# Summing the 16 states of a Mamba scan by accumulating DMAs issued from GpSimd (and the edges, the top two and the clamps by other instructions)

## Chip, cores and metric

One core of a Trainium2 chip, float32 data throughout. The metric is device microseconds of one launch. Three runs of the kernel before gave 5624.48, 5624.8 and 5625.91 us.

## What is computed

Input x is 4 sequences of 2048 tokens of 512 channels. One layer, with six modulation rows made from a small condition vector:

```python
h = layernorm(x) * (1 + ca) + sa
x = x + ga * mamba(h)
h = layernorm(x) * (1 + cb) + sb
x = x + gb * moe(h)          # 8 experts, the top two of 8 sigmoid scores, and one shared expert

# mamba: z = h @ W_in; val, gate = split(z); val = silu(conv3(val)); B, C, Delta from val
def step(h, inp):
    a_t, b_t, c_t, u_t = inp
    h = a_t * h + b_t * u_t[..., None]
    y_t = jnp.sum(h * c_t[:, None, :], axis=-1)     # the sum over 16 states
    return (h, y_t)
# out = y * silu(gate) @ W_out + residual
```

The recurrence runs over 2048 tokens for 512 channels with 16 states each. The change touches the sum over states, the gate times y, the 3-tap convolution's edges, the clamps on Delta, and the choice of the top two experts.

## The kernel before

**Tiling.** Tokens go in 16 blocks of 512 (`NQ`). The recurrence goes in 32 units (`NU`) of 128 channels by 1024 tokens. Each unit has 16 states (`N`), so there are 512 states (`NC`) in all, numbered c. Everything in a unit is a tile of 128x1024.

**The order is written by hand.** A window H has 32 slots r, and slot (H, r) belongs to state c = 32 H + r, so a window is two units. Five functions write one slot for their engine: `sync_slot`, `act_window` (four slots together), `pe_slot`, `dve_slot`, `pool_slot`. Windows run from -3 to 18. Beside the states, window H carries the Mamba front part of token block H+2 or H+3 (normalise, value and gate projections, convolution, Delta) and the expert part of block H-2 or H-3. All engines work through their queues in order, and all ordering between engines is by counted semaphores.

**One state.** TensorE broadcasts a row of B into two PSUM banks (L1047). VectorE multiplies it by u (L1068, `times_u`), by 1+abar (L1074, `times_abar`), by a weight (L1081, `times_weight`), by a ratio (L1088, `times_ratio`), then runs the scan (L1098) into `hs[c % 2]`. ScalarE makes the weights' parts by Square, Ln, Exp, Tanh and Exp (L672 to L687). GpSimd multiplies two of them (L1299, `weight`). SyncE loads the row of C, broadcast to 128 partitions (`Cb`, L501), two states deep.

**The sum.** `times_C` of GpSimd (L1277 to L1292) waits for the scan, multiplies `hs[c % 2]` by `Cb` in place (L1284), and from a unit's second state on adds it to `ysum` (L1291). `hs` has two buffers, so scan c waits for the addition of state c-2 (L1096); `y_added` counts the 15 additions of a unit. In slot r, GpSimd's queue has `times_C(c-1)`, then `weight(c+2)`, then other work such as the expert gating (L1311). VectorE's queue has `times_weight(c)`, `early()`, `times_ratio(c)`, `times_u(c+1)`, `scan(c)`, `times_abar(c+1)`, `late()`.

**The gate.** In slots 1 and 17 `early()` calls `gate_y` (L1118): it waits for the whole sum of the unit before, then `gy = ysum * gy`. SyncE stores `gy` in slots 2 and 18 (L531), and the first addition of the next unit waits for it to be done (`y_gated`).

**Other work that the change touches.** `take_val` (L710, ScalarE) takes a projection out of PSUM, and `convolve` (L1151, L1154) adds the outer taps and then the two edge columns (L1158, L1159). `softplus` (L1138, L1140, L1143) makes Delta and clamps it from both sides. `inverse_delta` (L772) takes its Ln. `softplus_exp` has an Abs and an Exp (L736, L738). `top_two` (L1179 to L1202) ranks 8 scores by comparing all pairs, in slot 14, after ScalarE's Sigmoid (L816). Four PSUM banks are given to projection and expert matmuls by a small planner (`bank_held_to`, `taken`): each job takes the bank that is planned to be free first and waits for that bank's last reader. SyncE's queue issues all the DMAs of this kernel; `us` (L521) is loaded once per unit, into one buffer.

Of the kernel before, what the change touches and what calls it, by code (L numbers as in the profile page):

```python
# [12 lines left out]
P = 128  # L13
# [5 lines left out]
Y_CAP = 1e18  # L19


def adaln_mamba_moe(nc, x, W_val, W_gate, taps, W_BC, W_deltaT, delta_base, W_tau, A_log, W_out, gate_W, W1, b1, W2, b2,
                    route_scale, cT, wmod, ident, onehot, earlier, out):
# [49 lines left out]
    with ExitStack() as ctx:  # L73
# [28 lines left out]
        low = sb("low", [P, E, E])  # L102
# [40 lines left out]
        rank = sb("rank", [P, TPB, E])  # L143
# [13 lines left out]
        xnf = flat(xn[:])  # L157
        pre, lnw, tt1 = hTv, xa[:], uu[:]
        above = xnf[:, 0:TPB * E * E].rearrange("p (t e f) -> p t e f", t=TPB, e=E)
        ties = xnf[:, TPB * E * E:2 * TPB * E * E].rearrange("p (t e f) -> p t e f", t=TPB, e=E)  # L160
# [37 lines left out]
        LOADS = 10  # L198
        with nc.Block() as block:
            @block.sync  # L200
            def _(sp):
# [19 lines left out]
                sp.dma_start(flat(low[:]), earlier.partition_broadcast(P)).then_inc(ld, 16)  # L221
# [69 lines left out]
            def _(dve):  # L291
# [32 lines left out]
                done(v.memset(gates[:, :, E:EX], 1.0))  # L324
                dve.wait_ge(a_done, 1)
# [53 lines left out]
        y_added, y_gated, carry_done = sem("y_added"), sem("y_gated"), sem("carry_done")  # L379
# [4 lines left out]
        tap_left, conv_done, conv_edges, b_split = (  # L384
            sem("tap_left"), sem("conv_done"), sem("conv_edges"), sem("b_split"))
# [4 lines left out]
        a_abs, a_exp, a_t, a_corr, a_ln, a_log1p, a_sum, delta_done = (  # L390
            sem("a_abs"), sem("a_exp"), sem("a_rounded"), sem("a_correction"), sem("a_ln"), sem("a_log1p"), sem("a_softplus"),
# [45 lines left out]
        def adds(c):  # L437
            return (N - 1) * (c // N) + c % N
# [222 lines left out]
        def act_window(act, H, w):  # L661
# [42 lines left out]
            def take_val(q, ms):  # L704
                if has(q):
                    ge(act, st_u, 16 * q)
                    ge(act, a_log1p, 2 * q)
                    for m in ms:
                        act.wait_ge(mm_val, G * q + m + 1)
                        s.activation(uu[:, m, :], ps[:, bank_of["val", q, m], :], ACT.Identity,  # L710
                                     scale=tapc[:, 1, m:m + 1]).then_inc(ev_val, 1)

            def silu_of_u(q):
                if has(q):
                    act.wait_ge(conv_edges, q + 1)
                    s.activation(uu[:], uu[:], ACT.Silu).then_inc(silu_u, 1)
# [14 lines left out]
            def softplus_exp(q, gp):  # L731
                if has(q):
# [5 lines left out]
                    s.activation(lnw[:, part, :], lnw[:, part, :], ACT.Exp, scale=-1.0).then_inc(a_exp, 1)  # L738

# [37 lines left out]
            def at(place):  # L777
# [30 lines left out]
                if w == 3:  # L808
# [5 lines left out]
                    if place == 0 and has(qf):  # L814
                        act.wait_ge(mm_log, qf + 1)
                        s.activation(flat(sco[:]), ps[:, bank_of["log", qf, 0], 0:TPB * E], ACT.Sigmoid).then_inc(ev_log, 1)  # L816
# [80 lines left out]
        def bank_held_to(j, at):  # L897
# [19 lines left out]
        def taken(j):  # L917
# [15 lines left out]
            if kind == "log":  # L933
                return ev_log, q + 1
# [120 lines left out]
        def dve_slot(dve, H, r):  # L1055
# [78 lines left out]
            def softplus(q, gp):  # L1134
                if has(q):
# [4 lines left out]
                    v.scalar_tensor_tensor(pre[:, part, :], pre[:, part, :], 0.0, lnw[:, part, :], ALU.max, ALU.add).then_inc(a_sum, 1)  # L1140
                    dve.wait_ge(a_sum, 2 * q + gp + 1)
                    for g in (2 * gp, 2 * gp + 1):
                        ins = v.tensor_scalar(pre[:, g, :], pre[:, g, :], delta_lo[:, g:g + 1], DELTA_HI, ALU.max, ALU.min)  # L1143
                    ins.then_inc(delta_done, 1)

            def convolve(q, m):
                if has(q):
                    i = G * q + m + 1
                    o = ps[:, bank_of["val", q, m], :]
                    dve.wait_ge(ev_val, i)  # L1150
# [28 lines left out]
            def top_two(q):  # L1179
                n = [0]  # L1180

                def step(ins):
                    n[0] += 1
                    ins.then_inc(f_top, 1)
                    dve.wait_ge(f_top, q * 8 + n[0])
# [269 lines left out]
```

## Time and profile before

| | |
|---|---|
| runs, median | 5624.8 us |
| profiled execution: its time / its span | 5628.1 us / 5626.3 us |
| granted TensorE clock, mean | 0.831 of full |
| busy, of the span | DVE 82%, POOL 77%, PE 72%, ACT 71% |
| busy share of the 16 DMA engines | 42% |
| first and last scan start | 275.9 us and 5234.1 us |

PE is TensorE, DVE is VectorE, ACT is ScalarE, POOL is GpSimd, SP is SyncE. The profile gives each group of instructions (one line, one engine, one shape) its total busy time, the mean of one, and the idle time of its engine just before. An instruction that is held up while it runs shows as a long one, not as idle time. The chain that ended last goes through all engines (POOL 25%, DVE 22%, PE 17%, ACT 9%).

### The profile page before, as it was taken

Reading aid. Unit: us, or ns where it says so; the run is one execution under the profiler, and the core shown is the slowest. Engines: PE = TensorE matmul, PEld = TensorE weight load, DVE = VectorE, ACT = ScalarE, POOL = GpSimd, SP = SyncE. Lnnn points to the kernel's source line nnn. Section 1 sums busy time; section 2 is a strip of 40 time slices with the busy share of each in tenths; the row PEclk is TensorE's granted clock in tenths of the full one; section 3 lists DMA queues with packets and bytes.
Section 4 is the critical chain, followed back from the end, with each engine's and each line's share of the span. In section 5 each row is a group of like instructions: output and inputs, shape, how many; then the busy total and the mean of one; then the engine's idle time right before and its main releaser. Section 6 shows DMA issues by size and latency. Waiting matters only on the chain.

```text
span 5626.3 us, 36241 instructions
## 1 busy us (share of the span) xinstructions
PE 4047.7 (72%) x9708; PEld 1692.7 (30%) x9708; DVE 4587.0 (82%) x3829; ACT 3994.2 (71%) x4039; POOL 4345.7 (77%) x2132
## 2 busy tenths in 40 slices
PE   7531415787777778687878878687877875858889
PEld 3210102333333323233333323233333322323343
DVE  1378799989999898998989899998989899998310
ACT  1576777787878877787878777787878777878211
POOL 0299988797888878797988878797988879898311
PEclk8765757888888889788988889788988887878989
DMA  4454524353444435343444435353434434343322
GB/s 135 150 206 165 203 98 166 113 177 123 154 140 150 154 123 182 114 172 131 154 137 149 155 125 180 116 171 133 154 137 149 149 118 148 118 151 122 112 95 71
DMA packets 274406, 802.25 MB, mean 143 GB/s; under 512 B 33173, under 2 KB 36117, under 8 KB 266902
## 3 DMA queue, kind: packets, MB, share of 16 engines
q1 hardware_dynamic: 274202, 799.94, 42.0%
q8 instruction: 78, 1.28, 0.1%
q14 instruction: 126, 1.03, 0.1%
HBM read 673.32 MB, written 126.51 MB: 142 GB/s over the span
## 4 chain that ended last, share of the span: by engine, by line
POOL 25%; issue 24%; DVE 22%; PE 17%; ACT 9%; DMA 1%; POOLq 0%; SPq 0%; DVEq 0%; ACTq 0%
POOL hs L1284 9%; POOL inv L1299 5%; PE ps L990 4%; PE ps L1036 4%; PE ps L1020 4%; POOL hid L1311 3%; DVE ps L1074 3%; DVE ps L1081 3%; DVE ps L1068 3%; POOL ysum L1291 2%; ACT inv L677 2%; DVE hT L1140 2%; PE ps L981 1%; DVE ps L1088 1%; DVE xa L1138 1%
## 5 line engine op out<-in xcount | busy, mean ns | idle before, releaser
L1284 POOL TENSOR_TENSOR hs<-hs,Cb 128x1024 f32<-128x1024 f32 x512 | 1226.0, 2395 | 267.7 <-DVE hs L1098 244.9
L1299 POOL TENSOR_TENSOR inv<-inv,th 128x1024 f32<-128x1024 f32 x512 | 1231.1, 2404 | 210.3 <-ACT th L684 209.8
L1020 PE MATMUL ps<-hf,w1r 128*128 128x512 f32 x2304 | 1159.6, 659 | 78.3 <-DMA w1r<-in_W 62.9
L1036 PE MATMUL ps<-w2r,hid 128*128 128x512 f32 x2304 | 1129.7, 644 | 29.1 <-ACT hid L758 28.1
L1291 POOL TENSOR_TENSOR ysum<-ysum,hs 128x1024 f32<-128x1024 f32 x448 | 1061.8, 2370 | 35.1
L1047 PE MATMUL ps<-Brow,pick 48*128 48x512 bf16 x1024 | 363.2, 440 | 864.7 <-DVE hs L1098 864.2
L684 ACT ACTIVATE th<-delta,halfA 128x1024 f32<-128x1024 f32 x512 | 583.0, 1139 | 383.0 <-POOL inv L1299 382.7
L1068 DVE TENSOR_TENSOR ps<-ps,us 128x1024 f32<-128x1024 f32 x512 | 627.5, 1226 | 257.8 <-PE ps L1047 153.0
L672 ACT ACTIVATE inv<-nrd,kappa 128x1024 f32<-128x1024 f32 x512 | 557.1, 1139 | 359.4 <-DVE ps L1081 355.5
L1020 PEld LDWEIGHTS ps<-hf,w1r 128*128 128x128 f32 x2304 | 473.5, 212 | 699.7 <-issue 673.3
L1081 DVE SCALAR_TENSOR_TENSOR ps<-ps,coef,inv 128x1024 f32<-128x1024 f32 x512 | 657.9, 1285 | 24.4 <-DVE ps L1074 1.4
L1088 DVE SCALAR_TENSOR_TENSOR ps<-nrd,inv_kappa,ps 128x1024 f32<-128x1024 f32 x512 | 658.9, 1287 | 13.9
L1036 PEld LDWEIGHTS ps<-w2r,hid 128*128 128x128 f32 x2304 | 458.4, 206 | 675.3 <-issue 628.5
L1098 DVE TENSOR_TENSOR_SCAN hs<-abar,ps 128x1024 f32<-128x1024 f32 x256 | 582.8, 2277 | 61.1 <-POOL ysum L1291 60.9
L1074 DVE SCALAR_TENSOR_TENSOR ps<-abar,ps 128x1024 f32<-128x1024 f32 x512 | 617.0, 1205 | 1.6 <-ACT abar L687 1.6
L1098 DVE TENSOR_TENSOR_SCAN hs<-abar,carry,ps 128x1024 f32<-128x1024 f32 x256 | 598.3, 2337 | 16.2 <-POOL ysum L1291 16.2
L687 ACT ACTIVATE abar<-delta,negA 128x1024 f32<-128x1024 f32 x512 | 581.4, 1136 | 17.0 <-DVE hs L1098 16.8
L677 ACT ACTIVATE inv<-inv,consts 128x1024 f32<-128x1024 f32 x512 | 550.4, 1138 | 1.7
L682 ACT ACTIVATE inv<-inv 128x1024 f32<-128x1024 f32 x512 | 536.3, 1047 | 1.6
L758 ACT ACTIVATE hid<-ps,b_sb 128x512 f32<-128x512 f32 x288 | 186.9, 677 | 389.3 <-PE ps L1020 389.3
L1311 POOL TENSOR_TENSOR hid<-hid,gbc 128x1024 f32<-128x1024 f32 x128 | 313.6, 2452 | 175.3 <-ACT hid L765 87.6
L1047 PEld LDWEIGHTS ps<-Brow,pick 48*128 48x128 bf16 x1024 | 59.2, 98 | 1230.8 <-DVE hs L1098 1037.4
(150 smaller groups left out, 4944.7 us busy)
## 6 DMA issues: line engine op xcount, KB each, us to landing
Cb<-c_rows SPq DMA_DIRECT2D x512, 512.0 KB, 4.2
w2r<-w_scaled SPq DMA_DIRECT2D x144, 512.0 KB, 6.4
w1r<-in_W SPq DMA_DIRECT2D x144, 512.0 KB, 3.6
gbc<-expert_gates SPq DMA_DIRECT2D x128, 256.0 KB, 3.7
aw<-in_W_val SPq DMA_DIRECT2D x64, 256.0 KB, 4.7
xa<-in_x SPq DMA_DIRECT2D x16, 1024.0 KB, 8.0
h_residual<-hT SPq DMA_DIRECT2D x16, 1024.0 KB, 7.2
aw<-in_W_gate SPq DMA_DIRECT2D x64, 256.0 KB, 4.5
```

The lines of the kernel that those rows point to most:

```text
L677: s.activation(inv[:, c % 6, :], inv[:, c % 6, :], ACT.Ln, bias=consts[:, 1:2]).then_inc(ln_done, 1)
L684: s.activation(th[:, c % 2, :], delta[:, u % 2, :], ACT.Tanh, scale=halfA[:, c % N, u % G:u % G + 1]).then_inc(th_done, 1)
L1020: mm = t.matmul(o, w1r[:, n % 2, k, h * P:(h + 1) * P], hf[:, k, :], start=(k == 0), stop=(k == G - 1))
L1036: mm = t.matmul(o, hid[:, e % HB, h, tt * P:(tt + 1) * P], w2r[:, e % 3, h, :], start=(grp < 2 and e % 3 == 0 and h == 0), stop=(e % 3 == ...
L1068: v.tensor_tensor(X(c), X(c), us[:], ALU.mult).then_inc(uB_done, 1)
L1074: v.scalar_tensor_tensor(X(c), abar[:, c % 4, :], 1.0, X(c), ALU.add, ALU.mult).then_inc(p1_done, 1)
L1081: v.scalar_tensor_tensor(X(c), X(c), coef[:, c % N, u % G:u % G + 1], inv[:, c % 6, :], ALU.mult, ALU.mult).then_inc(pw_done, 1)
L1088: v.scalar_tensor_tensor(X(c), nrd[:, u % 2, :], inv_kappa[:, c % N, u % G:u % G + 1], X(c), ALU.add, ALU.mult).then_inc(bu_done, 1)
L1098: v.tensor_tensor_scan(hs[:, c % 2, :], abar[:, c % 4, :], X(c), 0.0 if first else carry[:, u % G, c % N:c % N + 1], ALU.mult, ALU.add).th ...
L1284: gp_.tensor_tensor(hs[:, c % 2, :], hs[:, c % 2, :], Cb[:, c % 2, :], ALU.mult).then_inc(hC_done, 1)
L1291: gp_.tensor_tensor(ysum[:], hs[:, 1 - c % 2, :] if c % N == 1 else ysum[:], hs[:, c % 2, :], ALU.add).then_inc(y_added, 1)
L1299: gp_.tensor_tensor(inv[:, c % 6, :], inv[:, c % 6, :], th[:, c % 2, :], ALU.mult).then_inc(thinv_done, 1)
```

## The change

The sum from a unit's third state on is no longer an instruction of GpSimd but a DMA that adds `hs` into `ysum` in SBUF, issued from GpSimd's queue. Two semaphores take the place of `y_added`: `y_begun` (one addition per unit) and `y_summed` (16 per DMA, 14 DMAs per unit). Each DMA is issued only when the one before has landed. Scan c waits for the landing of state c-2. `gate_y` moves from `early()` to `late()` of the same slot.

Beside it: ScalarE adds the edge columns while it takes the value projection (three instructions for one). The lower clamp on Delta goes into the Ln as a bias and the upper one into the existing instruction, with a new Relu on ScalarE. The top two come from VectorE's `max` and `match_replace` on 8 scores instead of comparing all pairs, with the scores kept in their PSUM bank until the gates are done.

```diff
+        def sums(c):
+            return (N - 2) * (c // N) + c % N - 1
...
-                        s.activation(uu[:, m, :], ps[:, bank_of["val", q, m], :], ACT.Identity,
-                                     scale=tapc[:, 1, m:m + 1]).then_inc(ev_val, 1)
+                        o, middle = ps[:, bank_of["val", q, m], :], tapc[:, 1, m:m + 1]
+                        s.activation(uu[:, m, 1:T - 1], o[:, 1:T - 1], ACT.Identity, scale=middle).then_inc(ev_val, 1)
+                        s.activation(uu[:, m, 0:1], o[:, 0:1], ACT.Identity, scale=middle,
+                                     bias=vhalo[:, m, q:q + 1]).then_inc(ev_val, 1)
+                        s.activation(uu[:, m, T - 1:T], o[:, T - 1:T], ACT.Identity, scale=middle,
+                                     bias=vhalo[:, m, NQ + q:NQ + q + 1]).then_inc(ev_val, 1)
...
+                    s.activation(pre[:, part, :], pre[:, part, :], ACT.Relu).then_inc(a_relu, 1)
...
-                        s.activation(nrd[:, u % 2, :], delta[:, u % 2, :], ACT.Ln).then_inc(nr_ln, 1)
+                        s.activation(nrd[:, u % 2, :], delta[:, u % 2, :], ACT.Ln, bias=delta_lo[:, u % G:u % G + 1]).then_inc(nr_ln, 1)
...
-                        dve.wait_ge(y_added, adds(c - 1 if (c - 2) % N == 0 else c - 2))
+                        if (c - 2) % N < 2:
+                            dve.wait_ge(y_begun, unit(c - 2) + 1)
+                        else:
+                            dve.wait_ge(y_summed, 16 * sums(c - 2))
...
-                    dve.wait_ge(y_added, (N - 1) * (u + 1))
+                    dve.wait_ge(y_summed, 16 * (N - 2) * (u + 1))
...
-                    v.scalar_tensor_tensor(pre[:, part, :], pre[:, part, :], 0.0, lnw[:, part, :], ALU.max, ALU.add).then_inc(a_sum, 1)
-                    dve.wait_ge(a_sum, 2 * q + gp + 1)
-                    for g in (2 * gp, 2 * gp + 1):
-                        ins = v.tensor_scalar(pre[:, g, :], pre[:, g, :], delta_lo[:, g:g + 1], DELTA_HI, ALU.max, ALU.min)
-                    ins.then_inc(delta_done, 1)
+                    dve.wait_ge(a_relu, 2 * q + gp + 1)
+                    v.scalar_tensor_tensor(pre[:, part, :], pre[:, part, :], DELTA_HI, lnw[:, part, :], ALU.min, ALU.add).then_inc(delta_done, 1)
...
-                    if m == G - 1:
-                        dve.wait_ge(conv_done, i)
-                        v.tensor_tensor(uu[:, :, 0:1], uu[:, :, 0:1], vhalo[:, :, q:q + 1], ALU.add)
-                        v.tensor_tensor(uu[:, :, T - 1:T], uu[:, :, T - 1:T], vhalo[:, :, NQ + q:NQ + q + 1],
-                                        ALU.add).then_inc(conv_edges, 1)
...
-                step(v.tensor_scalar(sco[:], sco[:], rs_sb[:, 0:1], None, ALU.mult))
-                other = sco[:].unsqueeze(2).broadcast_to([P, TPB, E, E])
-                mine = sco[:].unsqueeze(3).broadcast_to([P, TPB, E, E])
-                v.tensor_tensor(above, other, mine, ALU.is_gt)
-                step(v.tensor_tensor(ties, other, mine, ALU.is_equal))
-                step(v.tensor_tensor(ties, ties, low[:].unsqueeze(1).broadcast_to([P, TPB, E, E]), ALU.mult))
-                step(v.tensor_tensor(above, above, ties, ALU.add))
-                step(v.tensor_reduce(rank[:], above, AX_X, ALU.add))
-                step(v.scalar_tensor_tensor(gates[:, :, 0:E], rank[:], 1.5, sco[:], ALU.is_lt, ALU.mult))
-                step(v.tensor_reduce(gsum[:], gates[:, :, 0:E], AX_X, ALU.add))
+                step(v.tensor_scalar(sco[:], score, rs_sb[:, 0:1], None, ALU.mult))
+                for tt in range(TPB):
+                    step(v.max(best[:, tt, :], sco[:, tt, :]), tt == TPB - 1)
+                step(v.tensor_reduce(chosen[:, :, 0:2], best[:, :, 0:2].unsqueeze(3), AX_X, ALU.add))
+                for tt in range(TPB):
+                    step(v.match_replace(rest[:, tt, :], chosen[:, tt, :], sco[:, tt, :], 0.0), tt == TPB - 1)
+                step(v.scalar_tensor_tensor(score, score, rs_sb[:, 0:1], rest[:], ALU.mult, ALU.subtract))
+                step(v.tensor_reduce(gsum[:], score, AX_X, ALU.add))
...
             def early():
-                if r in (1, 17):
-                    gate_y(c // N - 1)
...
             def late():
+                if r in (1, 17):
+                    gate_y(c // N - 1)
...
                     if c % N:
                         pool.wait_ge(hC_done, c + 1)
+                        ge(pool, y_summed, 16 * sums(c - 1) if c % N > 2 else 0)
                         if c % N == 1:
                             ge(pool, y_gated, u)
+                            gp_.tensor_tensor(ysum[:], hs[:, 1 - c % 2, :], hs[:, c % 2, :], ALU.add).then_inc(y_begun, 1)
                         else:
-                            pool.wait_ge(y_added, adds(c - 1))
-                        gp_.tensor_tensor(ysum[:], hs[:, 1 - c % 2, :] if c % N == 1 else ysum[:], hs[:, c % 2, :],
-                                          ALU.add).then_inc(y_added, 1)
+                            pool.wait_ge(y_begun, u + 1)
+                            gp_.dma_start(ysum[:], hs[:, c % 2, :], accum_op=ALU.add).then_inc(y_summed, 16)
```

In the planner, the scores' bank is planned to be held to slot 14.95 instead of 13.8, and its next job waits for `f_gates` instead of `ev_log`. One setup load (the table `low`) goes, and one memset comes.

## Rows read from the trace of the kernel before

**Rows 1.** Busy us of PE, PEld, DVE, ACT, POOL, first to last scan

```profile
276.00:5240.00 4964.00, 3526.23 (x8377) 1449.97 (x8376) 4476.83 (x3610) 3844.23 (x3859) 4263.38 (x2088) 0.83 0.43 147
```

**Rows 2.** Who VectorE waited for there: us in total, times, longest

```profile
DVE ps L1068 <- PE ps L1047: 153.0, 77, 4.9
...
DVE ps L1068 <- DMA us<-u_rows: 83.5, 17, 7.2
...
DVE hs L1098 <- POOL ysum L1291: 77.1, 59, 4.7
...
DVE gy L1118 <- POOL ysum L1291: 33.2, 14, 4.1
```

**Rows 3.** Two states at the quickest pace: start, us, engine

```profile
2337.36 2.35 DVE L1098 TENSOR_TENSOR_SCAN hs<-abar,carry,ps 128x1024 f32<-128x1024 f32 x1
...
2342.60 2.37 POOL L1284 TENSOR_TENSOR hs<-hs,Cb 128x1024 f32<-128x1024 f32 x1
...
2344.60 2.34 DVE L1098 TENSOR_TENSOR_SCAN hs<-abar,carry,ps 128x1024 f32<-128x1024 f32 x1
...
2345.00 0.32 SPq L501 DMA_DIRECT2D Cb<-c_rows  x1
```

**Rows 4.** Groups of instructions, GpSimd's product with C and its additions

```profile
L1284 POOL TENSOR_TENSOR hs<-hs,Cb 128x1024 f32<-128x1024 f32 x512 | 1226.0, 2395 | 267.7 <-DVE hs L1098 244.9
...
L1291 POOL TENSOR_TENSOR ysum<-ysum,hs 128x1024 f32<-128x1024 f32 x448 | 1061.8, 2370 | 35.1
```

**Rows 5.** Groups of instructions, VectorE's work that the change removes

```profile
L1143 DVE TENSOR_SCALAR hT<-hT,delta_lo 128x512 f32<-128x512 f32 x64 | 75.4, 1219 | 1.1
...
L1158 DVE TENSOR_TENSOR uu<-uu,vhalo 128x4 f32<-128x4 f32 x16 | 24.4, 1523 | 0.5
...
L1189 DVE TENSOR_SCALAR sco<-sco,rs_sb 128x32 f32<-128x32 f32 x16 | 22.0, 1378 | 28.1 <-ACT sco L816 28.1
...
L1193 DVE TENSOR_TENSOR xn<-sco 128x256 f32<-128x256 f32 x16 | 36.8, 2299 | 0.0
...
L1194 DVE TENSOR_TENSOR xn<-xn,low 128x256 f32<-128x256 f32 x16 | 35.1, 2195 | 0.5
...
L1192 DVE TENSOR_TENSOR xn<-sco 128x256 f32<-128x256 f32 x16 | 6.8, 425 | 0.6
...
L1197 DVE SCALAR_TENSOR_TENSOR gates<-rank,sco 128x32 f32<-128x32 f32 x16 | 3.1, 192 | 0.5
```

**Rows 6.** Groups of instructions, VectorE's work with two SBUF inputs of 128x1024

```profile
L1138 DVE TENSOR_TENSOR xa<-xa,uu 128x1024 f32<-128x1024 f32 x32 | 80.3, 2510 | 0.0
...
L1140 DVE SCALAR_TENSOR_TENSOR hT<-hT,xa 128x1024 f32<-128x1024 f32 x32 | 98.2, 3069 | 1.1
...
L1118 DVE TENSOR_TENSOR gy<-ysum,gy 128x1024 f32<-128x1024 f32 x32 | 75.8, 2367 | 41.4 <-POOL ysum L1291 41.4
```

**Rows 7.** Groups of instructions, ScalarE, the nearest to what it gets

```profile
L738 ACT ACTIVATE xa<-xa 128x1024 f32<-128x1024 f32 x32 | 33.8, 1057 | 1.0
...
L816 ACT ACTIVATE sco<-ps 128x32 f32<-128x32 f32 x16 | 3.2, 197 | 9.8 <-PE ps L1005 9.7
```

**Rows 8.** DMA queue and issues: KB each, median us to landing

```profile
q1 hardware_dynamic: 274202, 799.94, 42.0%
...
Cb<-c_rows SPq DMA_DIRECT2D x512, 512.0 KB, 4.2
...
h_residual<-hT SPq DMA_DIRECT2D x16, 1024.0 KB, 7.2
...
u_rows<-uu SPq DMA_DIRECT2D x16, 1024.0 KB, 10.0
...
delta_rows<-hT SPq DMA_DIRECT2D x32, 512.0 KB, 3.0
```

**Rows 9.** First and last of 33 scans of one window

```profile
2147.66 2.34 DVE L1098 TENSOR_TENSOR_SCAN hs<-abar,carry,ps 128x1024 f32<-128x1024 f32 x1
...
2466.73 2.34 DVE L1098 TENSOR_TENSOR_SCAN hs<-abar,carry,ps 128x1024 f32<-128x1024 f32 x1
```

More of the change, by code:

```diff
@@ L18 @@
 INV_GUARD = 1e-18
-Y_CAP = 1e18
+NO_SCORE = 3e38
+Y_CAP = 1e9
 def adaln_mamba_moe(nc, x, W_val, W_gate, taps, W_BC, W_deltaT, delta_base, W_tau, A_log, W_out, gate_W, W1, b1, W2, b2,
-                    route_scale, cT, wmod, ident, onehot, earlier, out):
+                    route_scale, cT, wmod, ident, onehot, out):
     NB, L, D = x.shape
@@ L101, in adaln_mamba_moe @@
         vhalo = sb("vhalo", [P, G, 2 * NQ])
-        low = sb("low", [P, E, E])
         b1_sb = sb("b1_sb", [P, EX * HT])
@@ L142, in adaln_mamba_moe @@
         sco = sb("sco", [P, TPB, E])
-        rank = sb("rank", [P, TPB, E])
+        best = sb("best", [P, TPB, E])
+        chosen = sb("chosen", [P, TPB, E])
+        rest = sb("rest", [P, TPB, E])
         gates = sb("gates", [P, TPB, EX])
@@ L197, in adaln_mamba_moe @@
         halo_c, halo_v, halo_sq, halo_mm = sem("halo_eps"), sem("halo_steps"), sem("halo_sqrt"), sem("halo_transposed")
-        LOADS = 10
+        LOADS = 9
         with nc.Block() as block:
@@ L220, in _ @@
                 sp.dma_start(pick[BROW:BROW + 3 * N, :], onehot).then_inc(ld, 16)
-                sp.dma_start(flat(low[:]), earlier.partition_broadcast(P)).then_inc(ld, 16)
                 sp.dma_start(b1_sb[:], b1.rearrange("(k p) -> p k", p=P)).then_inc(ld, 16)
@@ L324, in _ @@
                 done(v.memset(gates[:, :, E:EX], 1.0))
+                done(v.memset(chosen[:, :, 2:E], NO_SCORE))
                 dve.wait_ge(a_done, 1)
@@ L378, in adaln_mamba_moe @@
             sem("B_ready"), sem("uB_done"), sem("abar_plus_1_done"), sem("weighted_done"), sem("bu_done"), sem("scan_done"))
[L379 removed]
+        y_begun, y_summed, y_gated, carry_done = sem("y_begun"), sem("y_summed"), sem("y_gated"), sem("carry_done")
         ax_ld, a_stat, a_sqrt, a_rstd, a_xn = (
             sem("a_x_loaded"), sem("a_stats"), sem("a_sqrt"), sem("a_rstd"), sem("a_normalized"))
[L384 to L385 removed]
+        tap_left, conv_done, b_split = sem("tap_left"), sem("conv_done"), sem("b_split")
         aw_ld = [sem(f"a_weight_{i}_loaded") for i in range(AWB)]
@@ L389, in adaln_mamba_moe @@
         silu_u, silu_g = sem("silu_u"), sem("silu_gate")
-        a_abs, a_exp, a_t, a_corr, a_ln, a_log1p, a_sum, delta_done = (
-            sem("a_abs"), sem("a_exp"), sem("a_rounded"), sem("a_correction"), sem("a_ln"), sem("a_log1p"), sem("a_softplus"),
+        a_abs, a_exp, a_relu, a_t, a_corr, a_ln, a_log1p, delta_done = (
+            sem("a_abs"), sem("a_exp"), sem("a_relu"), sem("a_rounded"), sem("a_correction"), sem("a_ln"), sem("a_log1p"),
             sem("delta_done"))
@@ L815, in at @@
                         act.wait_ge(mm_log, qf + 1)
-                        s.activation(flat(sco[:]), ps[:, bank_of["log", qf, 0], 0:TPB * E], ACT.Sigmoid).then_inc(ev_log, 1)
+                        s.activation(ps[:, bank_of["log", qf, 0], 0:TPB * E], ps[:, bank_of["log", qf, 0], 0:TPB * E], ACT.Sigmoid).then_inc(ev_log, 1)
                     if place == 1:
@@ L933, in taken @@
             if kind == "log":
-                return ev_log, q + 1
+                return f_gates, q + 1
             if kind == "gT":
@@ L1149, in convolve @@
                     o = ps[:, bank_of["val", q, m], :]
-                    dve.wait_ge(ev_val, i)
+                    dve.wait_ge(ev_val, 3 * i)
                     v.scalar_tensor_tensor(uu[:, m, 1:T], o[:, 0:T - 1], tapc[:, 0, m:m + 1], uu[:, m, 1:T], ALU.mult,
@@ L1180, in top_two, with step @@
                 n = [0]
-                def step(ins):
+                def step(ins, wait=True):
                     n[0] += 1
                     ins.then_inc(f_top, 1)
-                    dve.wait_ge(f_top, q * 8 + n[0])
+                    if wait:
+                        dve.wait_ge(f_top, q * 13 + n[0])
+                score = ps[:, bank_of["log", q, 0], 0:TPB * E].rearrange("p (t e) -> p t e", t=TPB)
                 dve.wait_ge(ev_log, q + 1)
                 ge(dve, mm_gT, q)
-                step(v.tensor_scalar(sco[:], sco[:], rs_sb[:, 0:1], None, ALU.mult))
@@ L1199, in top_two @@
+                step(v.scalar_tensor_tensor(score, score, rs_sb[:, 0:1], rest[:], ALU.mult, ALU.subtract))
+                step(v.tensor_reduce(gsum[:], score, AX_X, ALU.add))
                 step(v.reciprocal(gsum[:], gsum[:]))
-                assert n[0] == 8
-                v.tensor_tensor(gates[:, :, 0:E], gates[:, :, 0:E], gsum[:].unsqueeze(2).broadcast_to([P, TPB, E]),
+                assert n[0] == 13
+                v.tensor_tensor(gates[:, :, 0:E], score, gsum[:].unsqueeze(2).broadcast_to([P, TPB, E]),
@@ L1442 @@
             _mybir.dt.np(_mybir.dt.bfloat16)),
-        "earlier": _np.tril(_np.ones((E, E), _np.float32), -1).reshape(E * E),
     }
```

9 lines of the change are left out of this document (2 added, 7 removed).

## The prediction, made blind

> **What bounds the kernel now.** I read the shares of busy time first, then the stretches, then the waits of VectorE, then the starts of the scans. From the first scan to the last there are 4964 us of the 5626. There VectorE is busy 4477 us (90%), GpSimd 4263 (86%), ScalarE 3844, TensorE 3526 [rows 1]. So VectorE sets the pace, with GpSimd close behind. VectorE idles 487 us. The largest parts are 153 for TensorE, 84 for the load of u, and only 77 + 33 for GpSimd's additions [rows 2]. The work outside the scans (662 us) hardly changes.
>
> Next, the pace. A state takes 4964 / 511 = 9.7 us on average, but that is a mixture. The quickest pace is 7.24 us from scan to scan [rows 3]; the slots with much other work on VectorE are long. Of the 511 intervals between scan starts, 196 are under 8 us, 135 are 8 to 9.7 and 99 are over 12. In the window of [rows 9] the 32 intervals add up to 319.07 us and are, from slot 0: 14.5, 9.6, 8.9, 12.5, 7.6, 8.8, 9.4, 8.2, 9.8, 9.5, 7.2, 9.8, 15.8, 13.1, 15.6, 7.6, 14.7, 7.3, 7.2, 18.1, 7.2, 7.6, 10.4, 7.6, 7.6, 8.2, 11.0, 7.2, 8.7, 9.0, 11.9, 7.6. I use it as the pattern of all 16 windows.
>
> **The change, part by part.**
>
> *Clamps.* 64 clamps of 1219 ns go: -75 us. The instruction before them stays one instruction. A Relu on ScalarE comes, 32 of about 1.06 us, as the Exp beside it [rows 5, 7]. ScalarE has 1120 us idle in the stretch; I take +10 for the places where VectorE waits for this chain.
>
> *Edges.* Two small additions per block go, 24.4 us and 2.6 for the second: -27 [rows 5]. ScalarE gets 128 one-column instructions of about 0.2 us, as its Sigmoid of 32 columns [rows 7]. They lie ahead of the convolution, which VectorE runs from slot 1 on. Bounds 0 and 26 us; I take +16.
>
> *Top two.* The old form is 22.0 + 36.8 + 35.1 + three like the 6.8 + four like the 3.1, in all 127 us [rows 5]. The new one is some 18 small instructions, if each match_replace counts as two; at 0.2 us they make 3.6 us a block, 58 us. So -69. The scores' bank is held 1.15 slots longer; the transposes of the gates behind it wait for the same event anyway: 0.
>
> *The additions.* 448 additions of 2.37 us, 1062 us, leave GpSimd [rows 4]. That by itself gives nothing, since VectorE is the bound, but two things follow. First, VectorE's instructions with two SBUF inputs are drawn out while GpSimd works: L1193 takes 2299 ns and L1192, of the same shape, 425 [rows 5]. From 192 ns at 32 columns and 425 at 256, 1024 columns should take 1.22 us; the three kinds of [rows 6] take 2.51, 3.07 and 2.37, an excess of 138 us. GpSimd's work falls by a quarter, so I take a quarter of it: -35 (bounds 0 and -138). Second, the 110 us of waiting for additions [rows 2]. `gate_y` moves behind the scan, so its wait of 33 us goes; what stands there next is GpSimd's product for state 1, which draws it out as before. Of the 77, I take back a quarter: in all -50 (bounds 0 and -110).
>
> *The new chain.* Each DMA is issued when the one before has landed, so a state can't be quicker than L, the time from issue to landing with what GpSimd needs to issue. Behind GpSimd's wait in its queue are the issue itself and `weight(c+2)`, which VectorE needs a slot later. Scan c waits for the landing of c-2. The trace has no accumulating DMA and none from GpSimd, so I bound L. **Below**: the quickest store of 512 KB lands in 3.0 us and SyncE's issue takes 0.32: 3.3 us [rows 3, 8]. **Above**: a DMA of 1024 KB takes up to 10.0 us and the addition that it replaces 2.37: 12.4 [rows 4, 8]. **Taken**: an accumulation has to read two streams of 512 KB, so the nearest row is the 1024 KB DMA at 7.2 us, SBUF as its source, plus 1.0 for the issue: 8.2 us.
>
> What L costs I work out on the window of [rows 9]. The scan of c is done and multiplied about 5.3 us after its start (2.34 + 2.37 + 0.6 of lateness). It lands at the later of this and the landing before, plus L. Scan c+2 starts at the later of the old distance and that landing. At the quickest pace two states take 2 x 7.24 = 14.5 us, so a landing has 14.5 - 5.3 = 9.2 us. So up to 8.5 nothing is lost. With the savings above put in their slots (slot 3: 1.7, slot 14: 4.5, slots 16 and 19: 3.7 each, in all 13.6 us a window), the window changes by -13.6 at L = 8.5, -11.9 at 9, -5.6 at 9.5, +3.0 at 10, +13.0 at 10.5, +23.4 at 11 and +46.9 at 12. By 16 windows: -218, -190, -90, +48, +208, +374 and +750 us. **The turning point is about 9.8 us.** Between ends of 3.3 and 12.4 this is the number that decides.
>
> The Trainium skill, "DMA: Bandwidth & Descriptors", section "Anatomy of one DMA", gives for a DMA issued by GpSimd about 2.0 us plus bytes / 436e3: an estimate of 3.2 us for 512 KB and 4.4 for two streams. By it L would be far from the turning point. The trace has 4.2 us for the 512 KB rows of C, issued by SyncE beside other transfers, so I hold the page's figure low here.
>
> *Traffic.* The queue moves 799.94 MB in 42.0% of 16 engines' time, that is 339 GB/s while busy, or 1.55 us for 512 KB [rows 8]. 448 accumulations of 1.55 to 3.1 us add 12 to 25% of the span to the 42%. The row of C is loaded at the same moment, when the product is done, but has two states' time. The load of u is the exposed one, one per unit: 32 x 1.5 us later is +48 as a bound; I take +40 with the weights.
>
> *Sum.* -75 + 10 - 27 + 16 - 69 - 35 - 50 + 40 + 0 = -190 us. Against the profiled execution's 5628.1 this makes 5438, and the median of the runs lies 3.3 us below it: **5435 us**.
>
> **Rivals.**
>
> *B, the chain of landings becomes the bound, slower (0.37).* The place is GpSimd's wait for the landing of c-1 and the scan's wait for c-2. It decides from L = 9.8 us. Against it stands 7.2 us for the same bytes read. For it stand the 10.0 us of another 1024 KB store, that every accumulation meets the load of a row of C on the same 16 engines, and that neither the adder nor GpSimd's making of descriptors has a price in this trace. At L = 11 the window sum gives +374, and with the other terms (-50 + 66) 6015 us; at 10.5 it gives 5850, and at 12 about 6390.
>
> *C, contention (0.10).* The accumulations leave VectorE alone but hold up the loads of u and of the expert weights by their own 3.1 us in place of 1.5: some 60 to 90 us dearer, about 5515 us. The waits for u (84 us) and TensorE's waits for weights would grow together.
>
> *D, the savings turn into other waits (0.06).* VectorE already waits 153 us for TensorE, whose queue has the expert matmuls in it [rows 2]. If the time freed in slots 14 to 19 only makes that wait longer, some 20 to 60 us are left: 5600 us.
>
> *E, VectorE keeps GpSimd from issuing (0.02).* L1193 shows the two engines shutting each other out. If that holds for the issue as well, the drawn out instructions of [rows 6], up to 3.1 us, delay a landing in 96 places; where the slot has no slack that makes up to 100 us, 5535 us. The Trainium skill, "SBUF — State Buffer", section "SBUF: two separate sides", says that a GpSimd DMA's descriptors wait while VectorE runs an instruction in a two-port mode. No row of this trace has such a DMA, so nothing here shows it yet.
>
> **How the numbers follow.** Measurements of this kernel can tell 0.2%, 11 us. My own case has 0.45, C 0.10, E 0.02, D 0.06 and B 0.37. D is partly within 11 us and B passes through zero: 0.05 for the same, 0.58 faster, 0.37 slower. The likeliest case's own range is 5350 to 5500. For 8 in 10 the range must reach into B: from 5350 (all of the 110 us of waits and more of the excess come back) to 6030 (L = 11). Beyond it lie about 0.13 above and 0.05 below.
>
> **What would show it.** Right: accumulations that land within 9 us of the last landing; next to no wait of scans for DMAs; quickest pace still 7.2 to 7.6 us; no clamp or edge rows; L1138 and L1140 somewhat shorter; GpSimd busy some 3300 us, waiting more. Wrong: scans or GpSimd waiting for ysum's DMAs in hundreds of places and intervals under 9 us gone (B), the wait for u doubled (C), or the wait for B's row on TensorE grown by over 100 us (D).

## The result and the profile after

The changed kernel takes 5480.95 us (median of four runs, 5478.18 to 5481.9), the kernel before beside it 5624.64. The ratio is 0.9743, with a 95% interval of 0.9726 to 0.976: **144 us faster**, against 190 us in the prediction (5435 us, range 5350 to 6030). The profiled execution took 5478.18 us with a span of 5476.4.

From the page of the changed kernel: busy time, the DMA queues, the chain that ended last by engine, and two kinds of DMA with their us from issue to landing.

```profile
PE 4017.3 (73%) x9708; PEld 1675.1 (31%) x9708; DVE 4403.8 (80%) x3862; ACT 4051.8 (74%) x4199; POOL 3658.4 (67%) x2132
...
q1 hardware_dynamic: 274058, 799.91, 44.3%
q0 software_dynamic: 64512, 234.91, 22.0%
...
DMA 23%; issue 19%; PE 17%; DVE 16%; ACT 12%; POOL 11%; POOLq 0%; SPq 0%; DVEq 0%; ACTq 0%
...
Cb<-c_rows SPq DMA_DIRECT2D x512, 512.0 KB, 4.9
ysum<-hs POOLq DMA_DIRECT2D x448, 512.0 KB, 6.6
```

VectorE's busy time fell by 183 us (4587.0 to 4403.8) and GpSimd's by 687; the 392 us in which it issues accumulations count as busy here. The chain now has 23% of DMA in it, and 22% is one kind, the accumulation. The groups of instructions that answer to [rows 4, 6], with GpSimd's weight and its issues:

```profile
L1298 POOL TENSOR_TENSOR inv<-inv,th 128x1024 f32<-128x1024 f32 x512 | 1331.2, 2600 | 275.3 <-ACT th L682 275.2
L1282 POOL TENSOR_TENSOR hs<-hs,Cb 128x1024 f32<-128x1024 f32 x512 | 1249.7, 2441 | 262.9 <-DVE hs L1104 227.6 <-DMA ysum<-hs 13.7
L1291 POOL DMA_DIRECT2D ysum<-hs x448 | 391.9, 875 | 509.9 <-issue 399.8 <-POOL hs L1282 91.9 <-ACT th L682 18.2
...
L1144 DVE TENSOR_TENSOR xa<-xa,uu 128x1024 f32<-128x1024 f32 x32 | 102.0, 3186 | 2.4 <-ACT xa L747 2.4
L1124 DVE TENSOR_TENSOR gy<-ysum,gy 128x1024 f32<-128x1024 f32 x32 | 82.0, 2562 | 8.0 <-DMA ysum<-hs 8.0
L1147 DVE SCALAR_TENSOR_TENSOR hT<-hT,xa 128x1024 f32<-128x1024 f32 x32 | 81.8, 2556 | 1.1
```

And who VectorE waited for, with total us, times and longest, to set beside [rows 2]:

```profile
DVE hs L1104 <- DMA ysum<-hs: 389.4, 128, 8.3
...
DVE bc_sb L1238 <- PE ps L984: 76.3, 14, 28.9
DVE ps L1071 <- PE ps L1050: 41.7, 31, 3.0
...
DVE ps L1071 <- DMA us<-u_rows: 37.0, 16, 20.5
...
DVE gy L1124 <- DMA ysum<-hs: 8.0, 1, 8.0
```

The scans wait 389 us for accumulations, where they waited 77 us for additions before. This table is of the whole execution, [rows 2] of the run of states. In the run of states alone the waits for TensorE's row of B fell from 153 to 42 us, those for its projection of B and C (L981 before, L984 after) from 84.5 to 18.5, and those for u from 84 to 16.5: a scan that waits gives these others time to be ready. So the difference of one kind of wait does not say what the DMAs cost. That takes experiments.

### The profile page after: what moved, and what is told of

It reads as the page before. It is cut to its first block, busy times and chain, and to the rows that moved or that the text cites. A ratio compares the mean times of both kernels' runs of the same rounds, so it can differ in the third digit from the quotient of the medians.

```text
span 5476.4 us, 36465 instructions
## 1 busy us (share of the span) xinstructions
PE 4017.3 (73%) x9708; PEld 1675.1 (31%) x9708; DVE 4403.8 (80%) x3862; ACT 4051.8 (74%) x4199; POOL 3658.4 (67%) x2132
## 3 DMA queue, kind: packets, MB, share of 16 engines
q1 hardware_dynamic: 274058, 799.91, 44.3%
q0 software_dynamic: 64512, 234.91, 22.0%
## 4 chain that ended last, share of the span: by engine, by line
DMA 23%; issue 19%; PE 17%; DVE 16%; ACT 12%; POOL 11%; POOLq 0%; SPq 0%; DVEq 0%; ACTq 0%
DMA ysum<-hs 22%; POOL hs L1282 6%; PE ps L1023 6%; DVE ps L1077 3%; DVE ps L1084 3%; PE ps L1039 3%; PE ps L993 3%; DVE ps L1071 3%; ACT inv L675 2%; POOL hid L1310 2%; DVE xa L1144 2%; POOL inv L1298 1%; ACT th L682 1%; DVE ps L1091 1%; PE ps L984 1%
## 5 line engine op out<-in xcount | busy, mean ns | idle before, releaser
L1298 POOL TENSOR_TENSOR inv<-inv,th 128x1024 f32<-128x1024 f32 x512 | 1331.2, 2600 | 275.3 <-ACT th L682 275.2
L1282 POOL TENSOR_TENSOR hs<-hs,Cb 128x1024 f32<-128x1024 f32 x512 | 1249.7, 2441 | 262.9 <-DVE hs L1104 227.6
L1039 PE MATMUL ps<-w2r,hid 128*128 128x512 f32 x2304 | 1142.9, 651 | 19.8 <-DVE x L1130 19.7
L1023 PE MATMUL ps<-hf,w1r 128*128 128x512 f32 x2304 | 1131.0, 646 | 2.9 <-DMA w1r<-in_W 2.3
L1291 POOL DMA_DIRECT2D ysum<-hs x448 | 391.9, 875 | 509.9 <-issue 399.8
L1310 POOL TENSOR_TENSOR hid<-hid,gbc 128x1024 f32<-128x1024 f32 x128 | 325.4, 2543 | 175.6 <-ACT hid L768 87.8
```

The source lines that it names most:

```text
L1023: mm = t.matmul(o, w1r[:, n % 2, k, h * P:(h + 1) * P], hf[:, k, :], start=(k == 0), stop=(k == G - 1))
L1039: mm = t.matmul(o, hid[:, e % HB, h, tt * P:(tt + 1) * P], w2r[:, e % 3, h, :], start=(grp < 2 and e % 3 == 0 and h == 0), stop=(e % 3 == ...
L1282: gp_.tensor_tensor(hs[:, c % 2, :], hs[:, c % 2, :], Cb[:, c % 2, :], ALU.mult).then_inc(hC_done, 1)
L1298: gp_.tensor_tensor(inv[:, c % 6, :], inv[:, c % 6, :], th[:, c % 2, :], ALU.mult).then_inc(thinv_done, 1)
```

## Where the waits lie

Scan c waits for the landing of state c-2. I took the idle time ahead of each scan by its slot (mean of windows 2 to 13, us). Eight slots have nearly all of it: slot 29 has 6.7, slot 12 5.5, slot 25 3.4, slot 0 2.2, slot 31 2.0, slots 11 and 24 1.2 each, and slot 21 0.8. The largest, in one window, on VectorE, GpSimd and SyncE (start, us, engine):

```profile
2351.02 2.34 DVE L1104 TENSOR_TENSOR_SCAN hs<-abar,carry,ps 128x1024 f32<-128x1024 f32 x1
...
2358.25 2.34 DVE L1104 TENSOR_TENSOR_SCAN hs<-abar,carry,ps 128x1024 f32<-128x1024 f32 x1
...
2372.29 2.35 DVE L1104 TENSOR_TENSOR_SCAN hs<-abar,carry,ps 128x1024 f32<-128x1024 f32 x1 [6.34 <-DMA ysum<-hs]
```

```profile
2351.69 0.88 POOL L1291 DMA_DIRECT2D ysum<-hs  x1 [0.30 <-POOL hs L1282]
2352.33 2.65 POOL L1298 TENSOR_TENSOR inv<-inv,th 128x1024 f32<-128x1024 f32 x1
2354.65 2.63 POOL L1330 TENSOR_TENSOR nrd<-nrd,gy 128x1024 f32<-128x1024 f32 x1
2356.98 2.62 POOL L1282 TENSOR_TENSOR hs<-hs,Cb 128x1024 f32<-128x1024 f32 x1
2359.90 0.87 POOL L1291 DMA_DIRECT2D ysum<-hs  x1 [0.30 <-POOL hs L1282]
...
2372.72 0.87 POOL L1291 DMA_DIRECT2D ysum<-hs  x1 [7.25 <-issue]
```

```profile
2359.99 0.43 SPq L622 DMA_DIRECT2D w1r<-w_out_scaled  x1
2360.47 0.43 SPq L624 DMA_DIRECT2D hf<-h_residual  x1
```

The scan of state 27 starts at 2351.02. Its product starts only 5.96 us later (2.5 us is the quickest), because GpSimd was still at the work of the state before: its accumulation, a weight (L1298) and a product for the inverse of Delta (L1330). Its accumulation is issued at 2359.90, and within 0.6 us SyncE issues two loads of 1 MB. The accumulation takes about 12 us instead of 6.6, and the scan of state 29 waits 6.34. Two things come together: a **late product** and **other loads in flight**. Slot 12 is the other pattern: the product of state 10 starts 11.6 us after its scan on average, since GpSimd stands ahead of it at `weight(12)`, waiting for ScalarE's Tanh.

How much other loads weigh can be read from all 448 accumulations, sorted by what SyncE's queue still had in flight 1.4 us after their issue, when the quickest of them move their first packets. The 33 that met nothing landed after 4.5 us in the median (4.5 to 5.2). The 177 that met only a row of C, mostly issued 0.3 us before them, took 6.4 us. The 151 that met a row of C and two or more further loads took 9.5 us. So the row of C goes with about 2 us of the usual landing.

## Experiments: the parts

**e1: the first part alone.** The changed kernel with GpSimd's own additions and `gate_y` in `early()`, as before the change.

```diff
-                            pool.wait_ge(y_begun, u + 1)
-                            gp_.dma_start(ysum[:], hs[:, c % 2, :], accum_op=ALU.add).then_inc(y_summed, 16)
+                            pool.wait_ge(y_added, adds(c - 1))
+                        gp_.tensor_tensor(ysum[:], hs[:, 1 - c % 2, :] if c % N == 1 else ysum[:], hs[:, c % 2, :],
+                                          ALU.add).then_inc(y_added, 1)
...
             def early():
+                if r in (1, 17):
+                    gate_y(c // N - 1)
```

> Only the edges, the top two and the clamps are changed; GpSimd adds all states itself and the gate stays ahead of the scan. Theory 1 (the gain of the changed kernel is the removed work of VectorE, and the accumulating DMAs give about as much in waits as they bring): VectorE's busy time falls by about 180 us and the time by 140 to 190 us, to 5435 to 5485 us. Rival (the DMAs bring a share of their own): the time falls by only 80 to 110 us, to 5515 to 5545 us, because GpSimd, still busy 4300 us, holds the scans up more often once VectorE is quicker (waits of scans for additions from 77 to over 150 us).

Measured: 5442.1 us, ratio 0.9673 (0.9657 to 0.9689). This is 182 us under before and 39 under the changed kernel. Busy time and VectorE's waits:

```profile
PE 4000.8 (74%) x9708; PEld 1675.6 (31%) x9708; DVE 4402.7 (81%) x3862; ACT 4052.1 (74%) x4199; POOL 4334.0 (80%) x2132
...
DVE hs L1101 <- POOL ysum L1286: 90.9, 66, 4.6
DVE gy L1121 <- POOL ysum L1286: 43.5, 16, 7.6
```

VectorE is as busy here (4402.7) as in the changed kernel, and the scans' wait for additions is only 14 us longer than before. So the gain is the work taken off VectorE, and the rival falls: GpSimd at 80% does not hold up the quicker VectorE. The other half of theory 1, that the DMAs give about as much as they bring, is not settled by this run; e9 decides it.

**e2: the sum alone**, on the kernel before, with the gate behind the scan and the diff's semaphores; edges, top two and clamps stay as before.

```diff
-                            pool.wait_ge(y_added, adds(c - 1))
-                        gp_.tensor_tensor(ysum[:], hs[:, 1 - c % 2, :] if c % N == 1 else ysum[:], hs[:, c % 2, :],
-                                          ALU.add).then_inc(y_added, 1)
+                            pool.wait_ge(y_begun, u + 1)
+                            gp_.dma_start(ysum[:], hs[:, c % 2, :], accum_op=ALU.add).then_inc(y_summed, 16)
```

> Only the sum by accumulating DMAs and the gate behind the scan, on the kernel before; edges, top two and clamps are the old ones. Theory 1: 5590 to 5660 us, scans waiting for DMAs some 300 us. Rival (the DMAs bring a share of their own): 5540 to 5580 us.

Measured: 5624.7 us, ratio 1.0001 (0.9992 to 1.0011), with 376.5 us of scans waiting for DMAs, where some 300 were expected. Alone it moves nothing.

**e4: the gate back ahead of the scan**, in the changed kernel.

```diff
             def early():
+                if r in (1, 17):
+                    gate_y(c // N - 1)
...
             def late():
-                if r in (1, 17):
-                    gate_y(c // N - 1)
```

> The changed kernel with gate_y back in early(), ahead of the scan of slots 1 and 17. Theory (moving it freed VectorE from waiting for the last landing): VectorE then waits for the landing of state 15 in each of 32 units, some 1 to 4 us each, 30 to 120 us more than 5481. Rival (the wait is hidden or only moves): within 15 us of 5481.

Measured: 5528.95 us, ratio 0.9831 (0.9816 to 0.9846), 48 us over the changed kernel. `gate_y` waits 46.1 us for landings instead of 8.0. The theory holds.

**e9: first part and the gate behind the scan, GpSimd adding**: e1 with `gate_y` in `late()`. The diff is against e1; against the changed kernel only the accumulating DMAs are replaced.

```diff
             def early():
-                if r in (1, 17):
-                    gate_y(c // N - 1)
...
             def late():
+                if r in (1, 17):
+                    gate_y(c // N - 1)
```

> The kernel with the first part alone (5442 us), with gate_y behind the scan of slots 1 and 17, as in the changed kernel, and GpSimd still adding. Theory 4 (moving the gate is what pays beside the first part, and the DMAs cost some 60 to 90 us): 5395 to 5425 us, the waits of gate_y (43.5 us) gone. Rival (with GpSimd adding, the wait only moves into the first addition of the unit, behind which the scan of state 2 waits): 5435 to 5455 us.

Measured: 5404.18 us, ratio 0.9605 (0.9589 to 0.9621). Busy time and VectorE's waits:

```profile
PE 3996.4 (74%) x9708; PEld 1674.0 (31%) x9708; DVE 4379.4 (81%) x3862; ACT 4051.4 (75%) x4199; POOL 4333.7 (80%) x2132
...
DVE hs L1101 <- POOL ysum L1286: 115.6, 67, 6.2
...
DVE gy L1121 <- POOL ysum L1286: 7.3, 1, 7.3
```

Theory 4 holds. Part of the gate's wait did move on, as its rival had it: the scans wait 25 us more than in e1 and the gate 36 less. So the change falls into three steps, each measured: **first part -182, gate behind the scan -38, accumulating DMAs +77**, in all -143 for 144 measured. On the kernel before, the second and third together gave 0 (e2), not +39. There VectorE has the old clamps and the old top two in slots 14, 16 and 19, so the parts don't simply add. Why not, no run shows.

## Experiments: what makes the DMAs cost

**e3: products ahead of weights.** In GpSimd's queue the weight of every fourth state goes behind the next product.

```diff
             times_C(c - 1)
-            weight(c + 2)
+            if (c + 1) % 4 == 0:
+                weight(c + 1)
+            if (c + 2) % 4 != 0:
+                weight(c + 2)
```

> The changed kernel with one reordering of GpSimd's queue: the weight of every fourth state, for which GpSimd waits for ScalarE's Tanh, stands behind the next product with C and its DMA instead of ahead of them. Theory 2 (the scans wait because the product with C is issued late, held up in GpSimd's queue by other waits, up to 11.6 us after the scan's start in slot 10): the product in slot 10 starts 2.5 to 4 us after its scan, the wait of 5.5 us in slot 12 goes, waits of scans for DMAs fall from 389 to about 200 to 280 us, and the time by 80 to 150 us. Rival (what counts is only the time of the DMA itself, 6.6 us median and 9 and more where other loads run): the waits stay at 350 us or more and the time within 20 us of 5481.

Measured: 5480.76 us, ratio 0.9745 (0.973 to 0.9759): no change, as the rival had it, though the scans' wait lies between the two forecasts. VectorE's waits:

```profile
DVE hs L1104 <- DMA ysum<-hs: 331.9, 136, 9.5
...
DVE bc_sb L1238 <- PE ps L984: 147.4, 14, 28.8
```

The product of state 10 starts 3.5 us after its scan instead of 11.6, and the wait in slot 12 falls from 5.5 to 0.4 us, as expected. But the wait for TensorE's B and C projection (L984), in the same slot, rises from 76 to 147 us, or from 18.5 to 89.7 in the run of states. Before the change that wait was there too (84.5 us in the run of states). So in slot 12 the wait for the DMA had only covered one for TensorE, and cost little. My theory was right about the mechanism and wrong about its price here.

**e5 and e6: fewer bytes beside the DMAs.** Both leave data out of the computation, so their results are wrong and only their times are used.

```diff
-                    sp.dma_start(hf[:], h_d[qx]).then_inc(h_ld, 16)
+                    if qx == 0:
+                        sp.dma_start(hf[:], h_d[qx]).then_inc(h_ld, 16)
+                    else:
+                        sp.dma_start(hf[:, 0, 0:16], h_d[qx][:, 0, 0:16]).then_inc(h_ld, 16)
```

The output weights in slot 28 get the same form, and in e6 those of the experts as well.

> The changed kernel, in which the two 1 MB loads of slot 28 (the output weights and the residual block) are cut to 64 bytes a partition from the second block on: these data are left out of the computation. Theory 3 (other loads in flight make the accumulating DMA slow): the accumulation of state 27, 11.9 us now, takes 5 to 8 us, the scans' wait of 6.7 us in slot 29 falls under 2 us, and the time by 40 to 110 us. Rival (the landing of state 27 is late because its product is, 7.2 us after its scan): the accumulation stays above 10 us or the wait above 4 us.

> As the one with small loads in slot 28, and the experts' weights are cut to 64 bytes a partition from the second block on as well. Theory 3: the median time from issue to landing falls from 6.6 to 5 to 6 us, none in the run of states takes over 9 us, the scans' waits for DMAs fall from 389 to under 120 us, and the time lies 100 to 250 us under 5481. Rival (product too late in GpSimd's queue): waits of 200 us and more stay, mainly in slots 12 and 24 to 25.

Measured: e5 5438.3 us, ratio 0.9667 (0.9651 to 0.9683). The accumulation of state 27 takes 6.9 us (mean) instead of 11.9, and the wait in slot 29 is 1.7 instead of 6.7. That is 43 us for two loads per window. But the wait in slot 0 rose from 2.2 to 4.6. e6 5419.89 us, ratio 0.9637 (0.9622 to 0.9651). VectorE's wait in it:

```profile
DVE hs L1116 <- DMA ysum<-hs: 320.6, 124, 8.0
```

So with the experts' loads gone too, 321 us of waits stay, where I had expected under 120. The time fell by 61, not by 100 or more, the median landing hardly moved (6.5 us), and the longest is still 11.7 us. Landings under load are one part; the late products are another and stay, and so do the rows of C, which no run here cut.

**e12: the control without accumulating DMAs**: e9 with the loads of e6 cut, each in this form. It leaves the same data out.

```diff
-                    sp.dma_start(w2r[:, p % 3], w2g_d[q // QPB, EXPERTS[p]]).then_inc(w2_ld[p % 3], 16)
+                    if q == 0:
+                        sp.dma_start(w2r[:, p % 3], w2g_d[q // QPB, EXPERTS[p]]).then_inc(w2_ld[p % 3], 16)
+                    else:
+                        sp.dma_start(w2r[:, p % 3, 0, 0:16], w2g_d[q // QPB, EXPERTS[p]][:, 0, 0:16]).then_inc(w2_ld[p % 3], 16)
```

> The control to the kernels with small loads: first part, gate behind the scan, GpSimd adding, no DMAs (5404 us), with the same loads of weights and of the residual block cut to 64 bytes a partition from the second block on, which leaves these data out of the computation. If the 61 us that the cut gave beside the DMAs came from the DMAs landing sooner, this one stays within 15 us of 5404. Rival (the cut helps through TensorE, which waits for its weights): it falls by 40 to 70 us as well, to 5335 to 5365.

Measured: 5392.99 us, ratio 0.9594 (0.9578 to 0.961), 11 us under e9. So of e6's 61 us about 50 come by way of the accumulations, if the two parts add. Of their cost of 77 us, that much is contention with these loads. The other 27 us no run takes apart. The record has three things for them: the late products, the rows of C, and VectorE itself, which is busy 24 us longer in the changed kernel than in e9 (4403.8 and 4379.4).

**e7 and e8: DMAs in some states only.** `summed(c)` gives the semaphore and count of either kind. In e7 GpSimd adds the states 7, 9, 10, 22, 23, 27, 29 and 30 of a window; in e8 all but 18 to 21, 24 to 26 and 28.

```diff
-                            pool.wait_ge(y_begun, u + 1)
-                            gp_.dma_start(ysum[:], hs[:, c % 2, :], accum_op=ALU.add).then_inc(y_summed, 16)
+                            pool.wait_ge(*summed(c - 1))
+                        if by_pool(c):
+                            gp_.tensor_tensor(ysum[:], hs[:, 1 - c % 2, :] if c % N == 1 else ysum[:], hs[:, c % 2, :],
+                                              ALU.add).then_inc(y_begun, 1)
+                        else:
+                            gp_.dma_start(ysum[:], hs[:, c % 2, :], accum_op=ALU.add).then_inc(y_summed, 16)
```

> The changed kernel, but GpSimd adds by itself in the eight slots whose landing comes last or next to last before a scan (states 7, 9, 10, 22, 23, 27, 29, 30 of 32), and DMAs add in the other 20. Theory 2 and 3 together: waits of the scans for sums fall from 389 to 100 to 200 us, and the time to 5400 to 5450 us, at or under the kernel with the first part alone (5442). Rival (what the DMAs relieve is nothing, any wait removed comes back as a wait for TensorE): 5440 to 5485 us.

> The changed kernel with DMAs in only eight states of 32 (18 to 21, 24 to 26, 28), where GpSimd was 9 to 13 us late in the kernel with the first part alone; GpSimd adds in all others. Theory: GpSimd's lateness in slots 24 to 31 falls from 10 to 13 us to 5 to 9 us, waits for sums stay under 130 us, time 5410 to 5445 us. Rival (GpSimd's lateness never reached VectorE): equal to the first part alone within 8 us, 5434 to 5450.

Measured: e7 5455.78 us, ratio 0.9697 (0.9683 to 0.9712); e8 5403.8 us, ratio 0.9607 (0.9591 to 0.9623). In e7 the scans' wait for DMAs fell to 251.6 us, where 100 to 200 were expected, and the time by 25. That lies in the rival's range, and the wait for L984 was back at 146.4 us. e8 seemed to beat the first part by 38 us through the DMAs, as its theory had it. But e9, run after it, has no DMA and the same time (5404.18): the gate did it, which e8 has in `late()` too. Lateness did fall in slots 26 to 30 (from about 12 us in e9 to between 7 and 10), and new waits of scans in slots 26 and 30 (4.7 and 1.5 us) gave it back. In all the scans of e8 wait 200 us for sums (124.0 for DMAs, 76.0 for additions), not under 130 as expected.

**e10 and e11: the better order.** e8 and e9, each with the reordering of e3.

> The kernel with DMAs in eight states (5404 us), with every fourth weight behind the next product with C. Theory 2 (late products make the landings late): the product of state 24 starts 4 to 6 us after its scan instead of 10.7, the scans' wait for DMAs falls from 124 to under 60 us, time 5350 to 5395 us. Rival (TensorE takes over each wait that goes, as it did in slot 12): 5395 to 5410 us.

> First part, gate behind the scan and the reordered weight, no DMAs. Theory 5 (with these three the DMAs have nothing left to give): at or under the kernel with DMAs in eight states and the same reordering, within 10 us. Rival (GpSimd needs the relief in slots 18 to 31): 15 to 40 us slower than that one, with waits of scans for additions over 100 us.

Measured: e10 5335.54 us, ratio 0.9486 (0.9472 to 0.95); e11 5319.56 us, ratio 0.946 (0.9446 to 0.9474). In e10 the product of state 24 starts 6.5 us after its scan instead of 10.7 and the scans' wait for DMAs falls from 124.0 to 62.7 us, each a little short of what theory 2 expected, while the time lies under its range of 5350 to 5395 us. Theory 2 holds. Without any DMA the kernel is 16 us faster than with eight states of them. Theory 5 holds, with a little more than I expected of it. The same reordering that gave nothing beside 28 accumulations a window gives 85 us where GpSimd adds. Busy time and VectorE's waits in e11:

```profile
PE 3969.6 (75%) x9708; PEld 1661.6 (31%) x9708; DVE 4365.4 (82%) x3862; ACT 4044.8 (76%) x4199; POOL 4323.5 (81%) x2132
...
DVE ps L1084 <- POOL inv L1294: 105.4, 43, 7.1
DVE ps L1071 <- PE ps L1050: 85.7, 40, 5.4
```

The scans' wait for additions is down to 28.4 us. What GpSimd is waited for now is the weight. GpSimd's own weights in e9 and then in e11:

```profile
L1294 POOL TENSOR_TENSOR inv<-inv,th 128x1024 f32<-128x1024 f32 x512 | 1236.9, 2416 | 188.6 <-ACT th L682 188.3
```

```profile
L1294 POOL TENSOR_TENSOR inv<-inv,th 128x1024 f32<-128x1024 f32 x512 | 1218.6, 2390 | 6.7 <-ACT th L682 6.7
```

With the product ahead of it, the weight no longer stands waiting for ScalarE's Tanh (188.6 us of idle time to 6.7), and the product does not wait with it. **e11 is the fastest version, 161 us under the changed kernel.**

The distances from scan to scan show it by slot (us, mean of windows 2 to 13; slot r is from the scan of state r to the next):

```
slot     0    1    10   11   12   24   25   26   27   28   29   30   31   all 32
before  13.8  8.9  7.2 10.8 16.2  7.8  8.7 11.1  7.3  8.9  8.2 12.8  7.6   316.4
after    8.5 10.8  8.5 14.5  9.9 11.1  9.4  7.3  7.6 14.3  7.6 10.9  9.9   306.4
e9       8.5 11.6  7.2 10.6 16.1  7.8  8.8 10.4  7.6  9.4  9.2 11.8  7.6   300.2
e11      8.5 10.5  7.2  9.3 16.4  7.6  8.3  7.5  9.8  7.6 11.1  9.1  8.3   293.7
```

From e9 to the changed kernel, slots 24 to 31 get 5.5 us longer in all (+3.3 in slot 24, +4.9 in slot 28, +2.3 in slot 31, while slots 26, 29 and 30 get shorter), and slots 19 to 23, not shown, 3.5. Slots 10 to 12 together get shorter by 1.0.

## Why the prediction was right, and where it was not

**The bound** was right: VectorE's work set the pace, and taking some of it away gave the gain: in e1 its busy time fell by 184 us and the time by 182.

**Clamps, edges, top two** were summed to -145 and measured -182 (e1). The top two is the larger part of the error: its new instructions take 40 us in all instead of 58, so -87 instead of -69. The +16 for the edges did not show. ScalarE's one-column instructions take 0.34 us, more than my 0.2, but the convolution's wait for them went from 39.6 to 38.3 us (41.3 in e1). The Relu (32 of 1040 ns) is hidden too: VectorE waits 2.4 us for the chain that it stands in.

**The gate** was right in kind: -33 for its wait, and the move alone is -38 (e1 to e9). The balance is another one: its wait fell by 36 us, 25 came back as waits of scans, and VectorE's busy time fell by 23.

**The drawn out instructions** were wrong: -35 predicted, and -17 for a quarter of the scans' waits. The three kinds of [rows 6] sum to 254.3 us before and to 265.8 after. In e9, with GpSimd adding, they are 236.0. One kind that I had not counted did get shorter, `uu<-xa` (51.9 us before, 50.5 in e9, 28.5 after), but `rstdA` and `rstdF` took back 20.6 of this against e9. In all VectorE is busy 24 us longer than in e9. GpSimd does less in the changed kernel, but VectorE's work got no shorter by it.

**The chain of landings** is the step that failed. The price of one DMA came out lower: 6.6 us in the median from the start of the issue to the landing, with the 0.87 us of the issue in it, where I took 8.2 (7.2 and 1.0). The walk along the window gave 0 us of loss up to 8.5 us, and the measured cost, with any relief in it, is 77 us (e9 to the changed kernel). It used one duration and one lateness for all states. But a landing takes 4.5 to 12.5 us, and a product starts 2.5 us after its scan in some slots and 11.6 in others. Rival B's mechanism works in a few slots of each window, long before the mean reaches the turning point. The lateness was there to be read before the change: in slots 10, 11 and 24 to 30 the product began 11 to 13 us after its scan.

**Traffic** was predicted at +40, by way of u and the weights. The wait for u fell instead (84 to 16.5 us in the run of states). The contention was real, some 50 us (e6 against e12), but it fell on the accumulations themselves.

**The signs.** No clamp or edge rows and a quickest pace of 7.2 us came as forecast. "Next to no wait of scans for DMAs" did not: there are 128 of them, 389 us, and GpSimd waits 400 us ahead of its issues. L1138 (now L1144) got longer, 2.51 to 3.19 us, and L1140 (now L1147) shorter, 3.07 to 2.56. GpSimd is busy 3658 us and not 3300, because the issues count.

So -190 predicted and -144 measured. By the measured steps: the first part -182 for -145; the gate -38 for -33; the DMAs with all that GpSimd's relief was to give +77, where -35, -17 and +40 make -12. The DMAs came out 89 us dearer than forecast, and the first part and the gate saved 42 us more than forecast, which hides almost half of it. That the total came so near was luck.

Rival B's time was far off, its place was not. D's condition did not come about in slots 14 to 19, since the wait for the row of B in e1 is 145 us for 153, but a removed wait did turn into one for TensorE in slot 12 (e3). For E, the issues took 1.39 us at the most and were not held for the 3.1 us of a drawn out instruction. Seven accumulations were issued 0.8 us before an L1147 that ran for 3.5 us, and landed after 4.5 to 6.2 us.

## What to carry to other kernels

Moving work from an engine that isn't the bound to a DMA can cost time, because a landing can take longer than the instruction it replaces (here 6.6 us against 2.37); judge it where a buffer's release is already latest, not by the mean. Before adding such a path, look at what stands ahead of the producer in its queue: putting the product ahead of a weight that waits for another engine gave 85 us for moving one call. Run a change's parts alone: here one part hid that another one costs 77 us.

## What was not expected of the hardware

An accumulating DMA within SBUF takes more of the DMA engines than this kernel's other transfers of as many bytes. The accumulations moved 234.91 MB in 22.0% of the engines' time, which is 195 GB/s while busy; SyncE's queue moved 799.91 MB in 44.3%, or 330 GB/s. An accumulation of 512 KB therefore occupies 2.7 us of all 16 engines against 1.6. The Trainium skill, "DMA: Bandwidth & Descriptors", section "Anatomy of one DMA", would give an estimate of 3.2 us for the whole DMA, and 4.4 if both streams that it reads are counted; the trace has 6.6 in the median and 4.5 where nothing else was in flight, and the measurement decides.

Issuing costs GpSimd 0.87 us, and 0.30 us of idle time between the product and the issue, so about 1.2 us stand in place of an addition of 2.37. The weight behind the issue seems to take longer (L1298 2600 ns in the mean, against 2416 in e9 behind an addition), but its record begins before that of the issue ends: 2352.33 against 2351.69 + 0.88 in the lines above. Taken from the end of the issue on, it is 2389 ns.
